# Reciprocals spread over partitions by DMA in place of one-hot products, and four output units formed inside the last attention block

## What is computed

```python
x = x + ssm_scan(layernorm(x))      # state-space layer
x = x + ffn(layernorm(x))           # sqrt((x@cos(theta'))**2 + (x@sin(phi'))**2)
x = x + attention(layernorm(x))     # 16 heads of 16, rope, softmax, @ Wo + bo
x = x + ffn(layernorm(x))           # the same FFN weights
```

## Time and profile before

| | us |
|---|---|
| median of three runs | 3463.47 (3461.51 to 3465.16) |
| profiled execution, its own time | 3460.53 |
| its span, first to last instruction | 3458.8 |
| PE busy | 3288.3 (95% of the span) |
| DVE busy | 3242.6 (94%) |
| ACT busy | 2701.5 (78%) |
| POOL busy | 810.4 (23%) |
| mean granted clock of TensorE | 0.989 |

### The profile page before, as it was taken

One profiled execution on the slowest core, in us unless ns is written; L12 is line 12 of the kernel. 1 busy time (PEld: TensorE's weight loads), 2 busy tenths in 40 slices (PEclk: granted clock), 3 DMA queues, 4 the chain that ended last, 5 costly groups with the idle time before them and its releaser, 6 DMA issues.

```text
span 3458.8 us, 59198 instructions
## 1 busy us (share of the span) xinstructions
PE 3288.3 (95%) x22596; PEld 1189.6 (34%) x22596; DVE 3242.6 (94%) x4953; ACT 2701.5 (78%) x4973; POOL 810.4 (23%) x698
## 2 busy tenths in 40 slices
PE   7777778979999999999999999999999999999999
PEld 3222222533333333333333333333333333333334
DVE  7999998589999999999999999999999999999943
ACT  5766666747888888888888888888888888888865
POOL 2899997752000000000000000000000000000004
PEclk9999999979999999999999999999999999999999
DMA  2000001142012020202020211202020202020011
GB/s 66 1 10 1 0 1 55 49 125 31 14 27 31 10 33 6 33 8 34 6 33 6 33 18 24 32 7 33 6 33 8 34 6 33 6 34 8 7 55 49
DMA packets 53677, 87.09 MB, mean 25 GB/s; under 512 B 13200, under 2 KB 40464, under 8 KB 49232
## 3 DMA queue, kind: packets, MB, share of 16 engines
q1 hardware_dynamic: 53200, 82.77, 12.6%
q10 hardware_dynamic: 192, 0.52, 0.1%
HBM read 53.37 MB, written 21.23 MB: 22 GB/s over the span
## 4 chain that ended last, share of the span: by engine, by line
PE 82%; DVE 11%; issue 4%; ACT 1%; POOL 0%; DMA 0%; SPq 0%; DVEq 0%; POOLq 0%; ACTq 0%
PE banks L1487 29%; PE banks L1444 16%; PE banks L1439 15%; PE banks L1402 11%; DVE arena L989 5%; PE banks L522 3%; DVE arena L958 3%; PE banks L1400 2%; PE banks L785 1%; DVE arena L969 1%; DVE arena L1660 1%; PE banks L187 1%; PE banks L777 1%; PE banks L1509 1%; PE banks L1498 0%
## 5 line engine op out<-in xcount | busy, mean ns | idle before, releaser
L1643 DVE TENSOR_REDUCE arena<-banks 128x1 f32<-128x512 f32 x4032 | 2504.2, 684 | 19.0 <-PE banks L1402 15.6
L1617 ACT ACTIVATE arena<-banks 128x512 f32<-128x512 f32 x4096 | 2114.9, 603 | 417.6 <-PE banks L1439 409.7
L1439 PE MATMUL banks<-arena 64*128 64x512 bf16 x4032 | 1246.6, 380 | 0.0
L1444 PE MATMUL banks<-arena 35*128 35x512 bf16 x4032 | 1207.9, 378 | 0.9 <-DMA arena<-max_rows 0.5
L1487 PE MATMUL banks<-arena 128*32 128x512 f32 x8192 | 1090.8, 605 | 0.0
L1400 PE MATMUL banks<-arena 64*128 64x512 bf16 x2048 | 789.4, 387 | 22.9 <-DVE arena L1660 20.2
L1402 PE MATMUL banks<-arena 64*128 64x512 bf16 x2048 | 787.4, 386 | 0.6 <-DVE arena L1643 0.6
L1439 PEld LDWEIGHTS banks<-arena 64*128 64x128 bf16 x4032 | 375.9, 93 | 392.0 <-PE banks L1444 7.9
L1402 PEld LDWEIGHTS banks<-arena 64*128 64x128 bf16 x2048 | 188.0, 92 | 796.6 <-DVE arena L1643 792.3
L1444 PEld LDWEIGHTS banks<-arena 35*128 35x128 bf16 x4032 | 357.6, 93 | 158.7 <-ACT arena L1617 9.5
L685 PE MATMUL banks<-arena 128*128 128x512 f32 x512 | 258.1, 628 | 107.4 <-DVE arena L958 107.2
(11 more groups left out here) (133 smaller groups left out, 1653.8 us busy)
## 6 DMA issues: line engine op xcount, KB each, us to landing
arena<-qk_parts SPq DMA_DIRECT2D x242, 128.0 KB, 7.1
qk_parts<-arena SPq DMA_DIRECT2D x32, 384.0 KB, 2.6
arena<-arena SPq DMA_DIRECT2D x63, 128.0 KB, 2.3
x_res<-in_x SPq DMA_DIRECT2D x8, 512.0 KB, 7.4
arena<-in_trig SPq DMA_DIRECT2D x2, 2048.0 KB, 8.1
arena<-qk_parts SPq DMA_DIRECT2D x64, 64.0 KB, 10.1
att_t<-arena SPq DMA_DIRECT2D x128, 32.0 KB
arena<-att_t SPq DMA_DIRECT2D x8, 512.0 KB, 5.3
```

What stands on the lines that cost most here:

```text
L1439: return nc.tensor.matmul(sc[:, (4 * t + j) % SB, :], k, q, start=(j == 1), stop=(j != 1))
L1444: return nc.tensor.matmul(sc[:, (4 * t + j) % SB, :], k, q, start=(j != 1), stop=(j == 1))
L1617: nc.scalar.activation(prob[:, t % PBUF, j * CH:(j + 1) * CH], sc[:, n % SB, :], ACT.Exp, scale=SCALE).then_inc(exp_done, 1)
L1643: nc.vector.tensor_reduce(part_max[:, b % 2, u // NC, u % NC:u % NC + 1], mx[:, unit_bank(b, u), :], AXX, ALU.max).then_inc(dve_read, 1)
```

## The change

The one-hot matrix, its products on PE and its semaphores go. In their place the reciprocals of a half are stored to DRAM and loaded back into `recip_rows` (over the values `v`, which are no longer needed) with a source broadcast over the 16 partitions of each head: 32 transfers a half, issued by SP. For half 0 this stands in SP's order between `store(NB - 2)` and `store(NB - 1)`, for half 1 after `load_weighed(1)`. `weigh_row` reads `recip_rows`. Output units 0 to 3 are formed in the last block, in steps 8, 10, 12 and 14, into the three `mx` banks. Output units 8 to 15 come two FFN units later than before (OUT_LAG), and the eight rows of half 1 stand in DVE's order at the start of u = 2.

```diff
+OUT_LAG = 2
+EARLY_OUT = 4
-    to_rows = place(mem, 32, [DH, QC, P])[0:H * QC]
+    recip_rows = place(mem, 136, [2, QC, DH, CH])
+    recip_loaded = make_sems(nc, ctx, "ao", " ".join(f"recip{i}" for i in range(4)))
+    def out_bank(i):
+        return mx[:, i % MB, :] if i < EARLY_OUT else sc[:, i % 2, :]
...
+        def spread_reciprocals(half):
+            sp.wait_ge(recip_ready, half + 1)
+            sp.dma_start(mem.recip[half], recip[:, half, :]).then_inc(recip_stored[half], 16)
+            sp.wait_ge(recip_stored[half], 16)
+            if half == 0:
+                sp.wait_ge(v_ready, H)
+            by_chunk = mem.recip[half].rearrange("(d h c) t -> h d c t", d=DH, c=QC)
+            for c in range(QC):
+                for h in range(H // DH):
+                    sp.dma_start(recip_rows[h * DK:(h + 1) * DK, half, c, :, :],
+                                 by_chunk[h:h + 1, :, c, :].broadcast_to([DK, DH, CH])
+                                 ).then_inc(recip_loaded[half * 2 + c // 2], 16)
...
         load_weighed(0)
         store(NB - 2)
+        spread_reciprocals(0)
         store(NB - 1, last=True)
...
         load_weighed(1)
+        spread_reciprocals(1)
...
-        nc.gpsimd.memset(to_rows, 0.0).then_inc(one_hot, 1)
-        pool.wait_ge(one_hot, 1)
-        v = to_rows.rearrange("p h c (a r) -> p h c a r", r=DK)
-        nc.gpsimd.affine_select(out=v, in_=v, compare_op=ALU.not_equal, fill=1.0, base=0,
...
         def out_unit(i):
             pe.wait_ge(att_ready, half * QC * DH + (first // TPC + 1) * DH)
-            if i >= 2:
+            if i >= EARLY_OUT + 2:
                 pe.wait_ge(o_added, i - 1)
+            elif i >= MB and i < EARLY_OUT:
+                pe.wait_ge(o_added, i - MB + 1)
...
             kp = t - (STEPS - BS)
-            if kp % 2 and kp > 0:
-                recip_row(kp // 2)
+            if kp >= BS - 2 * EARLY_OUT and kp % 2 == 0:
+                out_unit((kp - BS) // 2 + EARLY_OUT)
...
-        for i in range(NU_F // 2):
+        for i in range(EARLY_OUT, NU_F // 2):
             out_unit(i)
-        for r in range(QC * DH, 2 * QC * DH):
-            recip_row(r)
         pe.wait_ge(acc_read, NB)
+        pe.wait_ge(o_added, EARLY_OUT)
         units.pe_turn(pe, 0)
-        pe.wait_ge(att_ready, 2 * QC * DH)
         for u in range(NU_F):
             units.pe_products(pe, u)
-            if u < NU_F // 2:
-                out_unit(NU_F // 2 + u)
+            if u >= OUT_LAG and u < NU_F // 2 + OUT_LAG:
+                out_unit(NU_F // 2 + u - OUT_LAG)
...
         def weigh_row(r):
             if dh == 0:
                 dve.wait_ge(att_loaded[half * QC + c], 16)
-            dve.wait_ge(recip_rows_ready, r + 1)
+                if c % 2 == 0:
+                    dve.wait_ge(recip_loaded[half * 2 + c // 2], 16 * 2 * (H // DH))
             att = att_half[half][:, dh, c * CH:(c + 1) * CH]
-            nc.vector.tensor_tensor(att, mx[:, r % MB, :], att, ALU.mult).then_inc(att_ready, 1)
+            nc.vector.tensor_tensor(att, recip_rows[:, half, c, dh, :], att, ALU.mult).then_inc(att_ready, 1)
...
         for u in range(NU_F):
+            if u == OUT_LAG:
+                for r in range(QC * DH, 2 * QC * DH):
+                    weigh_row(r)
             if u + 3 < NU_F:
                 dve.wait_ge(o_added, u + 4)
                 units.dve_stats(dve, u + 3)
             if u + 2 < NU_F:
                 units.dve_scale(dve, u + 2)
-            if u < NU_F // 2:
-                add_out(NU_F // 2 + u)
+            if u >= OUT_LAG and u < NU_F // 2 + OUT_LAG:
+                add_out(NU_F // 2 + u - OUT_LAG)
```

More of the change, by code:

```diff
@@ L1188, in attention @@
         ri=lambda u: banks[:, 2 + 4 * (u % 2):4 + 4 * (u % 2), :].rearrange("p k (a d) -> p k a d", a=2))
-    (one_hot, bias_added, sums_loaded0, sums_loaded1, recip_ready, recip_rows_ready, att_ready, o_ready,
+    (bias_added, sums_loaded0, sums_loaded1, recip_ready, recip_stored0, recip_stored1, att_ready, o_ready,
      o_added, out_stored) = make_sems(
-        nc, ctx, "ao", "onehot bias sumsloaded0 sumsloaded1 recip rows att o added stored")
-    sums_loaded = (sums_loaded0, sums_loaded1)
+        nc, ctx, "ao", "bias sumsloaded0 sumsloaded1 recip recipstored0 recipstored1 att o added stored")
+    sums_loaded, recip_stored = (sums_loaded0, sums_loaded1), (recip_stored0, recip_stored1)
     att_loaded = make_sems(nc, ctx, "ao", " ".join(f"att{i}" for i in range(NC)))
+    recip_loaded = make_sems(nc, ctx, "ao", " ".join(f"recip{i}" for i in range(4)))
     (first_loaded, rest_loaded, rows_loaded, ones_set, v_ready, first_ready, first_read, even_ready, odd_ready, dve_read,
@@ L1351, in gpsimd @@
         split_max(0)
-        nc.gpsimd.memset(to_rows, 0.0).then_inc(one_hot, 1)
-        pool.wait_ge(one_hot, 1)
-        v = to_rows.rearrange("p h c (a r) -> p h c a r", r=DK)
-        nc.gpsimd.affine_select(out=v, in_=v, compare_op=ALU.not_equal, fill=1.0, base=0,
-                                pattern=[[-QC * H // DH, DH], [-1, QC], [-QC, H // DH], [0, DK]],
-                                channel_multiplier=1).then_inc(one_hot, 1)
         for i in range(NC):
@@ L1490, in weigh @@
             last.then_inc(pv_done, 1)
[L1492 to L1499, removed]
         def out_unit(i):
@@ L1504, in out_unit @@
             pe.wait_ge(att_ready, half * QC * DH + (first // TPC + 1) * DH)
-            if i >= 2:
+            if i >= EARLY_OUT + 2:
                 pe.wait_ge(o_added, i - 1)
+            elif i >= MB and i < EARLY_OUT:
+                pe.wait_ge(o_added, i - MB + 1)
             for k in range(UT):
                 for h in range(DH):
-                    last = nc.tensor.matmul(sc[:, i % 2, k * D:(k + 1) * D],
+                    last = nc.tensor.matmul(out_bank(i)[:, k * D:(k + 1) * D],
                                             att_half[half][:, h, (first + k) * P:(first + k + 1) * P],
@@ L1687, in add_out @@
             xs = mem.x[:, i * UT:(i + 1) * UT, :]
-            nc.vector.tensor_tensor(xs, sc[:, i % 2, :].rearrange("p (k d) -> p k d", k=UT), xs,
+            nc.vector.tensor_tensor(xs, out_bank(i).rearrange("p (k d) -> p k d", k=UT), xs,
                                     ALU.add).then_inc(o_added, 1)
@@ L1702, in vector @@
         dve.wait_ge(o_added, 3)
+        add_out(4)
         units.dve_scale(dve, 0)
@@ L1705, in vector @@
         units.dve_stats(dve, 2)
-        add_out(4)
-        add_out(5)
+        for i in range(5, NU_F // 2):
+            add_out(i)
         reciprocals(1)
[L1709 to L1712, removed]
         for u in range(NU_F):
+            if u == OUT_LAG:
+                for r in range(QC * DH, 2 * QC * DH):
+                    weigh_row(r)
             if u + 3 < NU_F:
@@ L1758, in hybrid_kernel @@
         mem.att_t = nc.dram_tensor("att_t", [D, S], F32, kind="Internal").ap()
+        mem.recip = nc.dram_tensor("att_recip", [2, H * QC, CH], F32, kind="Internal").ap()
         mem.sums = nc.dram_tensor("att_sums", [2, H * QC, CH], F32, kind="Internal").ap()
```

## The result

The changed kernel takes 3469.76 us (median of 20 runs, 3466.44 to 3477.11), the kernel before 3462.82 us (20 runs). The ratio is 1.0021, 95% interval 1.0015 to 1.0027: 6.9 us slower. That it is slower is clear of the noise; whether by more than 0.2% is not, since the measured value lies on that border. The profiled execution of the changed kernel has a span of 3469.3 us against 3458.8, 10.5 more. So where I compare whole traces I count from that issue; the last one stands just ahead of the last block, and the end of the block is counted from there.

A forecast was written before the change was run, and what follows sets the result against it. PE's own work was taken to bound the kernel. A lag of +7.5 us from late transfers and +3.4 for the clock gave +10.9 on the median of 3463.47: 3474.4 us, range 3465 to 3484 for 8 in 10.

The forecast's parts named there:

- What is removed: On PE, sixteen one-hot products around the last block and a 0.6 us idle go: 16.1 us.
- the ceiling of 15: Largest gain if no transfer were late: removed PE work less what ACT's pace keeps, about -15 us, 3448.5.
- The first half's chain: Last block: store and spread transfers on SP make PE idle 5.0 us before output unit 0; block ends 4.8 us later.
- the pace p: Time between landings of two spread transfers, the larger of issue and movement: 0.55 us, ends 0.46 and 0.64.
- ACT too slow: ACT's exponentials in the last block, taken at 2.10 us a step, set PE's pace up to kp = 8.
- The second half: After the block PE idles 6.0 us before output unit 8, 11.5 before unit 3's products; lag +7.5 us.
- the forecast case: Main case: p 0.50 to 0.64, clock lost at least once; +3 to +15.5 us, chance 0.70.
- the formula 46p - 17.8: Lag at the products of unit 3, kept to the end, before any clock loss; +7.5 us at p = 0.55.
- the clock: Granted PE clock falls after the 5.0 and 11.5 us stalls, about 1.7 us each: +3.4 us, bounds 0 and 3.4.
- the partly hidden case: Rival for the transfer chain: p = 0.46 and no loss of clock, +3.4 us, 3466.8 us; chance 0.17.
- slower by more than 0.2%: Outcome of more than 6.9 us over the kernel before: the forecast case nearly whole and the worst case, chance 0.73.

The follow-up runs named there:

- b1: Changed kernel with half 0 spread ahead of SP's store, OUT_LAG = 4, and half 1's rows in two groups of four (u = 4, 6): 3446.54 us.
- b3: b1 with VectorE's second reciprocal moved from before unit 3's statistics to behind unit 2's scale: 3445.47 us.
- e1: Changed kernel with half 0's spreading ahead of the store of block NB - 2 in SP's order: 3464.81 us.
- e2: Changed kernel with four of half 1's eight row multiplications left at u = 2 and four moved to u = 4 on VectorE: 3458.55 us.
- c2: The changed kernel run and profiled once more, nothing altered: 3469.97 us.
- e3: Changed kernel with the same bytes in 16 transfers of 128 KB a half instead of 32 of 64 KB: 3471.58 us.
- e7: Changed kernel with PE multiplying unread products, 24 before output unit 0 and 6 before the products of unit 3: 3467.70 us.
- c1: e6 with four unread float32 products added on PE ahead of the one-hot products: 3461.08 us.
- e6: e1 with half 1 formed by one-hot products again, as in the kernel before, and no lag: 3468.04 us.
- e5: Changed kernel with no early output units; all eight of half 0 come after the last block: 3463.67 us.

## Why the prediction was right, and where it was off

The forecast was +10.9 us with slower as the likeliest sign (0.73); +6.9 was measured.

- What is removed and the ceiling of 15: right. b1 and b3 show the removed PE work as gain once nothing is late (14.7 and 15.6 in the traces).
- The first half's chain: right in place and kind. The wait before output unit 0 was 5.0 forecast, 5.96 and 4.36 in two traces. That the forecast lies between them is in part luck: the pace p was too slow, which made the wait too long, and ACT too slow, which brought PE to it most of a microsecond late and made it too short. e1 removes the wait by SP's order alone.
- The second half: both waits were where forecast. The one before output unit 8 was 3.5 to 3.7 us for 6.0, mostly because PE came to it 22.2 us after the end of the block, not 20.2 (the 1.6 us wait below). The one before the products of unit 3 was 7.6 to 8.8 us for 11.5. e2 shows that this one hangs on VectorE's order, as the step had it.
- The pace p is the mis-sized term: 0.55 forecast, 0.47 measured (32 issues in 14.78, 15.60, 14.78 and 14.79 us in the two traces). It lies below the forecast case's own 0.50 to 0.64. I let the full DMA engines of the earlier trace rows and the strided row decide, where the even intervals of the earlier trace rows, 0.46, were the nearest. With 0.468, their mean, the formula 46p - 17.8 gives +3.7, and with 3.4 for the clock +7.1, against +6.9. The pieces bear it out in c2: the end of the block is 5.1 us later than before (5.2 by the formula with one loss of clock), and the products of unit 3 begin 37.2 us after it (36.9). The first trace (+10.1) comes near the +10.9 by accident: there SP's store was slow, the first train began 2 us later than in c2, and the second train took 0.8 us more, which made up for the p that was too high. That e3 finds movement at its limit at 128 KB shows how near the other answer was.
- The clock: 1.7 us a wait charged, 1.8 to 2.4 seen behind the first and behind the last wait (the next group of matmuls counted in); filled waits (e7, c1) restore the rate. I held one fall of 1.7 us to be the worst that a wait does. In e6 it was 10 in the trace, 7 in the medians.
- Not foreseen: PE's 1.6 us wait for ACT's copy of unit 1, behind the second reciprocal on VectorE. In the changed kernel the later wait hides it; b3, which moves the reciprocal, has no such wait and is 1.1 us under b1 (the intervals overlap).
- The store of the second half's reciprocals landed 3.5 to 3.6 us after its issue, for 2.3 to 2.6 assumed. It made the second train a microsecond late.
- The row multiplications take 0.62 us apiece in a group of four, for the 0.69 assumed: 0.2 to 0.3 us on each group of four.

Of the rivals, the partly hidden case had the right p and the wrong clock. The chance of 0.73 for slower by more than 0.2% can be neither borne out nor refuted by a ratio of 1.0021 (1.0020 in c2).

## What to carry to other kernels

When work is taken off a full engine and handed to a transfer, write down the whole chain of the transfer (store, receipt, every issue on its queue, landing) and place its end beside the first instruction that needs it, on each in-order engine: here the changed kernel and b3 issue the same trains, and only the order on SP and VectorE and the lag on PE differ, 24 us apart. An in-order engine should take a late input behind what others wait for, and in as small groups as its consumers need. The waits of PE on this path that were 2.4 us (e5) to 8.8 us long had slowed work behind them, those of 1.7 us and less had none, so read the durations behind a wait as well as the wait.

## What the runs showed of the hardware

- A fallen clock can last long. Behind a wait of 4.22 us in e6 it was 0.50 for 14.0 us while PE worked without a break on 64-row float32 products, and 0.53 over the next 9.2 us of 128-row products with two breaks of 0.8 and 0.7 us. Behind the waits before output unit 0 and before the products of unit 3 in the changed kernel the durations were back to the usual after about 5 and 4.4 us. The same 64-row products run at full clock where the clock is full when they begin (c1, the kernel before). Why it stays low for so long in e6 is open.
- Transfers to 16 partitions with a broadcast source move like those with a plain one: 139 GB/s at half busy DMA engines with 64 KB issued every 0.47 us, 125 GB/s and full engines with 128 KB issued every 0.46 us; the plain loads of the earlier trace rows had 131 GB/s with full engines. Doubling the transfer halved the issue and gained nothing.
- VectorE's multiplication with both inputs in SBUF took 2.50 us for four, but 3.57 in e1 beside one addition of POOL and 4.65 in b1 beside two, which slowed too (b1's timeline):

```profile
3378.34 4.65 DVE L1690 TENSOR_TENSOR arena<-arena 128x512 f32<-128x512 f32 x4 [0.86 <-DMA arena<-att_recip]
3378.44 1.72 POOL L497 TENSOR_TENSOR x_res<-x_res,arena 128x512 f32<-128x512 f32 x1 [0.97 <-ACT arena L442]
```

POOL's addition of this shape takes 1.27 us elsewhere. The Trainium skill (SBUF — State Buffer, section Who interferes with whom) has a VectorE instruction with two SBUF inputs contend with a GpSimd instruction that reads SBUF. These rows agree in that both are longer; they do not show which one held the other up.
